# Moving the LayerNorm statistics behind the K/V work and the last mask product behind the query half, in a linear-attention plus tree-FFN layer on eight cores

## What is computed

```python
xn = layernorm(x)                               # x: (16, 2048, 1024)
# linear attention, 16 heads of 64
q, k, v = xn @ Wq.T + bq, xn @ Wk.T + bk, xn @ Wv.T + bv
q, k = fmap(q), fmap(k)                         # where(x > 0, x + 1, exp(x))
kv = einsum('bhnd,bhnm->bhdm', k, v); k_sum = k.sum(axis=2)
attn = einsum('bhnd,bhdm->bhnm', q, kv) / maximum(einsum('bhnd,bhd->bhn', q, k_sum), 1e-6)
attn = attn @ Wo.T + bo
# 8 decision trees of depth 7, 255 nodes each: only the nodes on the chosen path count
logits = xn @ W_in.T + b_in                     # 2040 columns
ffn = (silu(logits) * path_mask(logits > 0)) @ W_out.T
y = x + attn + ffn
```

## Time and profile before

| | us |
|---|---|
| time, median of 2 runs (1418.18 to 1419.85) | 1419.01 |
| the profiled execution: its time | 1425.49 |
| the profiled execution: span of its slowest core (core 1) | 1424.4 |
| spans of the 8 cores | 1408.5 to 1424.4 |
| phase 1, from the first V matmul to the last (core 1) | 48 to 383 |
| phase 2, from the first tile's logits to the end | 390 to 1424 |

### The profile page before, as it was taken

One profiled execution on the slowest core, in us unless ns is written; L12 is line 12 of the kernel. 1 busy time (PEld: TensorE's weight loads), 2 busy tenths in 40 slices (PEclk: granted clock), 3 DMA queues, 4 the chain that ended last, 5 costly groups with the idle time before them and its releaser, 6 DMA issues.

```text
span 1424.4 us, 18302 instructions; the slowest of 8 cores (1408.5 to 1424.4 us)
## 1 busy us (share of the span) xinstructions
PE 1206.5 (85%) x6784; PEld 552.7 (39%) x6784; DVE 668.1 (47%) x1399; ACT 461.6 (32%) x609; POOL 8.5 (1%) x15
## 2 busy tenths in 40 slices
PE   1799998999878888888888888888888888888895
PEld 0233433433324444444334444443344444434442
DVE  3256556556334444444444444455445444544452
ACT  2354544454313332222223322222233222222321
POOL 1000000000000000000000000000000000000000
PEclk9899999999978999999988999999899999988998
DMA  9991011111161100110000000100000011000000
GB/s 183 175 176 60 30 60 31 59 60 45 17 102 30 30 31 30 43 47 30 30 30 30 31 30 34 56 30 30 30 30 30 30 39 50 30 30 30 31 15 30
DMA packets 21607, 68.32 MB, mean 48 GB/s; under 512 B 2071, under 2 KB 2071, under 8 KB 21520
## 3 DMA queue, kind: packets, MB, share of 16 engines
q1 hardware_dynamic: 14112, 50.40, 10.9%
q0 software_dynamic: 7408, 16.76, 7.8%
HBM read 67.13 MB, written 16.78 MB: 59 GB/s over the span
## 4 chain that ended last, share of the span: by engine, by line
PE 47%; DVE 29%; DMA 12%; issue 8%; ACT 2%; DVEq 1%; SPq 1%; POOL 0%; ACTq 0%; POOLq 0%
PE p_acc L745 16%; DMA s_x<-x 9%; PE p_acc L717 5%; PE p_acc L719 4%; PE p_tr L701 4%; DVE s_scr L543 3%; DVE s_qp L563 3%; DVE s_norm L547 3%; PE p_kq L352 3%; DMA s_wkv<-wvt 3%; DVE s_phiq L538 3%; DVE s_acts L516 3%; DVE s_masked L604 3%; PE p_kq L388 2%; PE p_v L352 2%
## 5 line engine op out<-in xcount | busy, mean ns | idle before, releaser
L482 PE MATMUL p_L<-s_win,s_xnt 128*128 128x510 bf16 x1024 | 234.4, 381 | 7.5 <-DVE s_acts L516 7.5
L745 PE MATMUL p_acc<-s_wkv,s_mT 128*128 128x512 bf16 (+1 forms) x1024 | 226.4, 379 | 0.0
L495 ACT ACTIVATE s_acts<-p_L 128x1020 bf16<-128x1020 f32 x64 | 66.3, 1037 | 303.4 <-PE p_L L487 303.4
L482 PEld LDWEIGHTS p_L<-s_win,s_xnt 128*128 128x128 bf16 x1024 | 97.4, 98 | 137.8 <-issue 25.1
L745 PEld LDWEIGHTS p_acc<-s_wkv,s_mT 128*128 128x128 bf16 (+1 forms) x1024 | 98.8, 98 | 114.0
L505 DVE TENSOR_SCALAR s_dn<-s_acts 128x1020 bf16<-128x1020 bf16 x32 | 13.7, 427 | 232.1 <-ACT s_acts L495 232.1
L662 PE MATMUL p_tr<-s_ident,s_qp 128*128 128x128 bf16 x128 | 16.2, 268 | 121.4 <-DVE s_qp L563 121.4
L717 PE MATMUL p_acc<-s_wo,s_ap 128*128 128x512 bf16 x256 | 111.0, 434 | 0.0
L719 PE MATMUL p_acc<-s_wo,s_ap 128*128 128x512 bf16 x256 | 106.8, 417 | 0.0
L352 PE MATMUL p_kq<-s_wkv,s_xnt 128*128 128x512 bf16 x344 | 84.3, 389 | 23.1 <-DVE s_v L406 11.8
L465 PE MATMUL p_acc<-s_wq,s_xnt 128*128 128x512 bf16 x256 | 99.1, 387 | 3.0 <-ACT s_xnt L271 3.0
(11 more groups left out here) (115 smaller groups left out, 1588.0 us busy)
## 6 DMA issues: line engine op xcount, KB each, us to landing
s_x<-x SPq DMA_DIRECT2D x64, 512.0 KB, 4.5
y<-s_out SPq DMA_DIRECT2D x32, 512.0 KB, 2.9
s_win<-wint POOLq DMA_DIRECT2D x1, 4080.0 KB, 98.0
s_wkv<-woutt POOLq DMA_DIRECT2D x1, 3840.0 KB, 29.7
s_wkv<-wkt POOLq DMA_DIRECT2D x1, 2048.0 KB, 26.5
s_wkv<-wvt POOLq DMA_DIRECT2D x1, 2048.0 KB, 42.9
s_wq<-wqt POOLq DMA_DIRECT2D x1, 2048.0 KB, 54.8
s_wo<-wot POOLq DMA_DIRECT2D x1, 2048.0 KB, 67.1
```

The costliest lines, as they stand in the source:

```text
L482: T.matmul(p_L[:, 512 * k4:512 * k4 + 510], lhs, s_win[:, WIDTH * c + 510 * kk:WIDTH * c + 510 * (kk + 1)], start=(c == 0), stop=False)
L495: i = S.activation(s_acts[pb][:, 1020 * phase:1020 * (phase + 1)].rearrange("p (b c) -> p b c", b=2), srcL, AF.Tanh, scale=0.5)
L745: i = T.matmul(acc[:, 512 * half:512 * (half + 1)], lhs, s_wkv[0:kj, 1024 * j + 512 * half: 1024 * j + 512 * (half + 1)], start=False, sto ...
```

## The change

Two edits. In phase 1 the block with `emit_sums(t+3)`, `emit_pair` and `emit_xnstt` moves from the top of the iteration to its end, behind `phik` of tile t; `emit_xnstt(t+3)` now follows `emit_xnstt(t+2)` directly. In phase 2 `emit_mask_final` moves behind the second half of the query work. No instruction is added or removed.

```diff
@@ phase 1, for t in range(NT)
-        pend_stt3 = None
-        if t + 3 < NT:
-            sums_ev[t + 3] = emit_sums(t + 3, ev_xl[t + 3])
-            if t % 2 == 0:
-                ev_y = emit_pair(t + 2, sums_ev[t + 2], sums_ev[t + 3])
-                ev_stt[t + 2] = emit_xnstt(t + 2, ev_y)
-                pend_stt3 = ev_y
-
         em.wait("T", ev_xnTe, ev_wk, ev_brows, war_bank[r0], war_bank[r1])
@@ after emit_xnt(t + 1, ...)
-        if pend_stt3 is not None:
-            ev_stt[t + 3] = emit_xnstt(t + 3, pend_stt3)
@@ after phik of tile t
         pending_kv = (t, buf, ev_phik, ev_vb)
+
+        if t + 3 < NT:
+            sums_ev[t + 3] = emit_sums(t + 3, ev_xl[t + 3])
+            if t % 2 == 0:
+                ev_y = emit_pair(t + 2, sums_ev[t + 2], sums_ev[t + 3])
+                ev_stt[t + 2] = emit_xnstt(t + 2, ev_y)
+                ev_stt[t + 3] = emit_xnstt(t + 3, ev_y)
@@ phase 2
         ev_phiq0, ev_qp0 = emit_phiq_half(t, 0, cur["ev_e2"], cur["ev_qmm"])
+        ev_phiq1, ev_qp1 = emit_phiq_half(t, 1, None, None)
         ev_mk = emit_mask_final(t, cur["mlev"], cur["silu"])
-        ev_phiq1, ev_qp1 = emit_phiq_half(t, 1, None, None)
```

## The result

The changed kernel takes 1475.2 us against 1421.0: a ratio of 1.0373 (95% interval 1.0353 to 1.0394), 53 us more (here and below a difference is the ratio times 1420 us). It was forecast at 1432, with a range from 1392 to 1460. The direction of each edit was right, one plus and one minus; their sizes were not, and the error sits almost wholly in the clock.

What follows compares the result with a forecast made beforehand. Phase 1 was taken as bound by PE, phase 2 by a loop through several engines. +71.7 +25.5 -20.9 -2.4 -44.8 -13 -3 = +13.1 us on the median 1419.0 gave 1432 us, range 1392 to 1460.

Steps and rivals of the forecast that it cites:

- The waits: Phase 1, PE before the transposes of the normalized tile: 15 new waits of 4.78 us each, 71.7 us added.
- the waits of K on the V copy: Phase 1, PE before the K matmuls: these waits on DVE's late V copy would go, 20.9 us gained.
- the mask product: Phase 2, DVE: moved behind the second query half, it takes 1.40 us off each of 32 tiles, 44.8 us gained.
- Rivals C and D: C: phase 1 pair chain covered after all, 1335 us, chance 0.04. D: phase 2 mask product late for L701, 1454 us, 0.04.
- the few microseconds of the start: Start of phase 1: two x loads come later than wv, so the first V matmul waits less, 3 us gained.
- The clock term of phase 1: Phase 1, PE behind each new wait: half-rate work loses 1.70 us, 15 times, 25.5 us added (0 to 36.8).
- The ceiling: Phase 1: the clock's price per new wait would be at most 2.45 us, 36.8 us in all.
- The clock term of phase 2: Phase 2, PE: shorter idle time before L662 wins back a quarter of 52 us, 13 us gained (0 to 52).
- Rival B: Phase 2: the 2.1 us gap before L662 leaves the clock up, 52 us gained in place of 13, 1393 us; chance 0.14.
- The reservation in the text: Phase 2, behind the gap before L662: small pieces with gaps and 16 transposes stay, so only a quarter was taken as gained.
- The 52 us put down for the clock's whole price in phase 2: Phase 2: 3.3 us of busy PE at about half clock lose 1.6 us per tile, 52 us in all.
- Rival A: Phase 1 waits each cost the clock 2.45 us, phase 2 gets none back, 1459 us; chance 0.20.

Runs made afterwards that it cites:

- p1_newton3: Only the phase 1 edit on the kernel before, with three rounds of Newton's iteration in the pair chain in place of four; ratio 1.0402 to the kernel before.
- b_fill: The kernel before with 16 added matmuls per tile, results overwritten, inside PE's phase 2 wait before L662; ratio 0.9664 to the kernel before.
- p2_fill5: Only the phase 2 edit on the kernel before, with 5 added matmuls per tile before L662, results overwritten; ratio 0.9520 to the kernel before, 1352 us.
- p2_only: The kernel before with only the phase 2 edit, the mask product moved behind the second query half; ratio 0.9796 to the kernel before.

## Why the prediction was wrong, step by step

*The waits were right.* 4.78 us each was forecast, 4.65 measured, 15 of them; the waits of K on the V copy are gone; the mask product gives 44 us when the clock is held up, against 44.8, and stays covered by 0.7 us. Rivals C and D are refuted by the rows above. wv landed 38.8 us after its issue (core 3) where 42.9 were seen before (core 1), which fits the few microseconds of the start.

*The clock term of phase 1 is the step that failed first.* The text took 1.70 us per wait, with a ceiling of 2.45, and reasoned that "a longer wait uses up more of the slow time while PE has nothing to do". Measured: 2.80 per wait, 42 us in place of 25.5, above the ceiling of 36.8. The ceiling was no ceiling: it came from one wait of 3.87 us, and the runs with 2.58, 3.65 and 4.65 us show the mean price rising with the wait, 1.6, 2.1, 2.8. `p1_newton3` also shows equal waits priced 1 us apart, so two samples of one odd event, 2.45 and 1.70, could bound nothing.

*The clock term of phase 2 had the wrong sign.* 13 us were taken as gained; about 16 were lost. The shorter wait did not lift the clock, it went from 0.93 to 0.90. Rival B supposed that the 2.1 us gap would be harmless; it was not, and even 1.4 us in the same place left only 0.97. The reservation in the text, that the thin stretch stays, was right, but should have let the gain go to nothing or below. Half-rate time costs only where PE has work, and the idle time that vanished could cover some of it; how much of the 16 us that is, no run tells. That the slow time also grew (0.93 to 0.90 by stretch, more stretches of the long kind) is measured; why the shorter tile meets it worse is not settled by these runs. The 52 us put down for the clock's whole price in phase 2 came close to the 48 that `b_fill` gave, with some luck: they count 3.3 us of one tile's long stretch, times 32.

*The sum again with what was measured:* +69.7 + 42 - 23.3 - 44.8 + 16 - 3 = +56.6, against 53. The two clock terms are off by 16.5 and 29 us, 45 together; less the 2 us by which the waits came out shorter that is 43, and the miss is 40 (53 against 13); the rest is within the intervals. Rival A named the right mechanism for phase 1 (1459 us) and stayed short because it held phase 2's clock for unchanged and its price under the same ceiling.

*The rule of the Trainium skill* that was weighed (TensorE: Matmul & The Clock Gate, "Why this matters for your kernels", that only long gaps between bursts throw the clock back) does not hold for phase 2 here: with 2.3 us of idle time per tile in front of transposes the clock was 0.90. That page's remark on transposes ("Part 4: PE-mode transpose") fits what `p2_fill5` shows, though no run here tests transposes by themselves.

## What to carry to other kernels

When an edit leaves PE idle or takes idle time away, give the clock a term of its own with both signs open, and don't cap it with one event of the old trace; a filled kernel, with useless matmuls in the wait, measures it directly. When a block moves past another on an in-order engine, ask in which iteration its product is wanted: here the pair chain changed its parity, and the wait went from nothing to 4.65 us. And where a short chain of one engine sets a loop, look at what in its queue waits for something that nobody needs yet: here the normalizing, which waits for its load, worth 170 us once it stood behind the queries.

## What the runs showed of the hardware

Adding 10 or 16 matmuls per tile whose result is thrown away made the kernels 63 and 48 us faster, since the clock stayed at 1.00. The price of an idle gap is not set by its length alone: gaps of up to 1.3 us between full matmuls cost nothing (phase 1 before, 0.99 to 1.00), gaps of 1.4 us in front of transposes and small products left 0.97, gaps of 2.3 us there 0.90 to 0.93 by core and run (0.90 or 0.91 on seven cores of `p2_only`), and gaps of 3.8 us at the same place 0.92 or 0.93.
